# Graph attention on one core: the softmax's second pair of segmented scans replaced by two masked passes with precomputed tables

## The chip, the cores and the metric

The program runs on one core of one Trainium2 chip. The metric is the device time of one execution in microseconds; lower is better. A time given for a version is the median of its runs.

## The reference, cut to what matters

2500 nodes with 512 channels (8 heads of 64), 40000 edges sorted by their destination, two layers of attention over the edges, then a small MLP with layer norms. Everything is float32. The part that the change concerns is the softmax over all edges of one destination:

```python
for l in range(L):
    ...
    a = (q[dst] * k[src]).sum(-1) * scale
    amax = jax.ops.segment_max(a, dst, num_segments=N)
    ...
    e = jnp.exp(a - amax[dst])
    denom = jax.ops.segment_sum(e, dst, num_segments=N)
    alpha = e / (denom[dst] + 1e-16)
    agg = jax.ops.segment_sum(alpha[:, :, None] * v[src], dst, num_segments=N).reshape(N, C)
    x = agg + (x @ Ws[l] + bs[l]) + enc
```

## The kernel before, in words

The edges are cut into 176 steps of 256 edges (two tiles of 128), each step belonging to one block of 128 destination nodes; there are 20 blocks. The program is a sequence of stages with a barrier of all engines behind most of them (`give_back`, L98):

1. `first_keys` (L154) computes the rows k of the first layer, block by block (20 of them): TensorE turns and multiplies, ScalarE takes the high parts, VectorE the low parts (`low_part`, L435) and the results (`take_keys`, L445), and SyncE stores (L260, L263). Between the blocks VectorE builds the tables of steps (`between`, L581): after block 12 it spreads the destination ("key") of every edge, the keys are transposed by TensorE and copied back by ScalarE (L389) as `key_s`, [128 x 2816]. The 128 partitions are 16 chunks of the edge list times 8 heads; the 2816 columns are the edges of a chunk in order. After block 16 `mark_starts` (L556) compares each key with the one ahead of it, after block 17 `scale_starts` (L559) turns the result into 0 or -1e30 (`fresh`), and SyncE stores it to HBM (L271). After the last block `link_chunks` (L561) notes which chunks share a segment with their neighbours. GpSimd has little to do here: one low part (L283), four indirect DMAs and two casts (L292, L293). SyncE ends the stage by waiting for all stores (L272 to L278).
2. `score`, once for each layer, gathers k rows by indirect DMAs from GpSimd's queue (L657) and computes the scores of all edges, `k.edge`.
3. `soften_collect` (L1000), once for each layer, has two parts in one block of engine programs.
   - The softmax (L1293 to L1329): VectorE sorts the scores into chunk order, TensorE transposes them into PSUM (`big`), and VectorE runs two segmented max scans of 2816 columns: `fwd` forward and `bwd` backward, each from PSUM with the flags `fresh` from SBUF (L1303, L1304; all scans have the line of the helper, L1290). The maxima at the chunk ends go through TensorE and two tiny scans over the chunks, and come back as `carry_col`, the value that enters each chunk from either side. Then both long scans are run again, starting from `carry_col` (L1318, L1319), and the maximum of the two is each edge's segment maximum. Six pieces of up to 512 columns follow: maximum (L1325), scores minus maximum (L1329), exponential on ScalarE (L1469), transposition back on TensorE (L1222), copy to `k.edge` on ScalarE (L1475).
   - The collection, 176 steps: GpSimd gathers the v rows of a step by two indirect DMAs of 128 rows of 2 KB each (L657) into a ring of 16 steps. It starts on this at the beginning of the stage, beside the softmax, and waits when all 16 slots are full, until VectorE has used the first. VectorE weighs a step's rows with the exponentials (`weigh`, L1346), makes the one-hot matrices (L1333) and adds the sums to the block (L1360); TensorE multiplies (L1262). In the first layer VectorE also assembles each finished block as the next layer's x (L1382, L1387), and TensorE computes its k rows; SyncE loads what these need.
4. `finish` is the MLP with its norms. There GpSimd also does elementwise work (L1675) beside VectorE's (L1742).

`score` of layer 1 also splits weights on VectorE (L908) beside its gathers. The engines are ordered by semaphores alone; each engine runs its own list of instructions in the order of the code.

## Time and profile before

| what | value |
|---|---|
| runs | 2756.88, 2774.0, 2786.02 us |
| median | 2774.0 us |
| span of the profiled execution | 2242.0 us |
| own time of the profiled execution | not given by the page |
| VectorE (DVE) busy | 2018.6 us, 90% |
| TensorE (PE) busy | 1875.4 us, 84% |
| GpSimd (POOL) busy | 1506.2 us, 67% |
| ScalarE (ACT) busy | 539.5 us, 24% |

The span goes from the first to the last instruction of one profiled execution. The runs are timed from outside and hold what lies around the instructions as well. Times in the rows are in us from the span's start. The two softmax parts lie at 559 to 605 us and 1506 to 1551 us, `first_keys` ends at 98 us.

### The profile page before, as it was taken

Reading aid. Unit: us, or ns where it says so; the run is one execution under the profiler, and the core shown is the slowest. Engines: PE = TensorE matmul, PEld = TensorE weight load, DVE = VectorE, ACT = ScalarE, POOL = GpSimd, SP = SyncE. Lnnn points to the kernel's source line nnn. Section 1 sums busy time; section 2 is a strip of 40 time slices with the busy share of each in tenths; the row PEclk is TensorE's granted clock in tenths of the full one; section 3 lists DMA queues with packets and bytes.
Section 4 is the critical chain, followed back from the end, with each engine's and each line's share of the span. In section 5 each row is a group of like instructions: output and inputs, shape, how many; then the busy total and the mean of one; then the engine's idle time right before and its main releaser. Section 6 shows DMA issues by size and latency. Waiting matters only on the chain. (4 is left out here: it accounts for less than half of the span.)

```text
span 2242.0 us, 30495 instructions
## 1 busy us (share of the span) xinstructions
PE 1875.4 (84%) x7660; PEld 1411.1 (63%) x7661; DVE 2018.6 (90%) x2398; ACT 539.5 (24%) x1070; POOL 1506.2 (67%) x1499
## 2 busy tenths in 40 slices
PE   7699999986489999996999899854998878768997
PEld 6566666663367777774666666633766555557776
DVE  7499999999899999993999999989999888889994
ACT  3133333332311111112333333332111000032222
POOL 1177777775677777774777777757777777657553
PEclk9899999997699999997999999966999999979999
DMA  8688888885778888886888888856777777641111
GB/s 317 241 268 289 291 288 280 287 288 175 223 220 262 264 263 266 263 259 231 248 284 279 291 291 280 286 176 199 211 210 210 210 210 211 186 164 57 57 48 45
DMA packets 201631, 511.52 MB, mean 228 GB/s; under 512 B 37915, under 2 KB 60571, under 8 KB 201190
## 3 DMA queue, kind: packets, MB, share of 16 engines
q0 software_dynamic: 112832, 369.71, 53.7%
q1 hardware_dynamic: 85862, 135.89, 17.6%
q10 hardware_dynamic: 2880, 5.24, 0.7%
q8 instruction: 25, 0.41, 0.1%
q14 instruction: 32, 0.26, 0.0%
HBM read 451.33 MB, written 59.06 MB: 228 GB/s over the span
## 5 line engine op out<-in xcount | busy, mean ns | idle before, releaser
L657 POOL DMA_INDIRECT coll_rows<-v_rows,coll_index x704 | 673.7, 957 | 223.2 <-issue 199.0
L657 POOL DMA_INDIRECT all_work<-k_rows,all_work x704 | 668.7, 950 | 226.8 <-issue 204.1
L1262 PE MATMUL coll_banks<-coll_ev,coll_hot 128*128 128x260 f32 x2816 | 684.8, 390 | 76.1 <-DVE coll_ev L1346 47.9
L1262 PEld LDWEIGHTS coll_banks<-coll_ev,coll_hot 128*128 128x128 f32 x2816 | 517.4, 190 | 222.5 <-DVE coll_ev L1346 99.2
L851 PE MATMUL score_q_ps<-score_q,score_hot 128*128 x1408 | 418.4, 422 | 108.7 <-DVE all_work L879 50.3
L1346 DVE TENSOR_TENSOR coll_ev<-coll_rows,coll_banks 128x1024 f32<-128x1024 f32 x352 | 425.7, 1210 | 38.7 <-DMA coll_rows<-v_rows,coll_index 37.6
L879 DVE TENSOR_TENSOR all_work<-score_q_ps,all_work 128x1024 f32<-128x1024 f32 x352 | 428.8, 1220 | 35.2 <-issue 8.0
L884 DVE TENSOR_REDUCE graph_edge<-all_work 128x1024 f32 (+1 forms) x352 | 421.7, 1208 | 0.0
L851 PEld LDWEIGHTS score_q_ps<-score_q,score_hot 128*128 128x128 f32 x1408 | 268.8, 199 | 214.9 <-issue 164.8
L959 ACT ACTIVATE score_hot<-score_local,all_iota_col 128x512 fp32r<-128x512 uint8 x176 | 127.3, 723 | 613.4 <-DVE all_work L879 581.5
L1360 DVE TENSOR_TENSOR all_work<-all_work,coll_banks 128x520 f32 x352 | 241.7, 687 | 5.5 <-PE coll_banks L1262 5.3
L1513 ACT ACTIVATE coll_ev<-coll_e_now 128x16 f32<-128x16 f32 x352 | 75.2, 215 | 635.9 <-PE coll_banks L1262 635.8
L633 PE MATMUL score_new_q<-graph_wq_hi,score_xt 128*128 128x512 f32 x320 | 109.9, 405 | 29.9 <-DMA score_xt<-x_turned 29.9
L962 ACT ACTIVATE score_hot<-score_hot,all_ones 128x512 fp32r<-128x512 f32 x176 | 127.3, 723 | 5.8
L633 PE MATMUL score_new_skip<-layer_w_skip_hi,score_xt 128*128 128x512 f32 x320 | 121.4, 422 | 1.3 <-DVE score_skip L897 1.3
L1333 DVE TENSOR_TENSOR coll_hot<-coll_banks,coll_local_up 128x512 f32<-128x512 f32 x176 | 119.7, 681 | 0.2
L1663 POOL TENSOR_TENSOR mlp_h_lo<-mlp_h_all,mlp_h_hi 128x512 fp32r<-128x512 f32 x40 | 65.3, 1637 | 72.6 <-ACT mlp_h_hi L1867 68.1
L633 PE MATMUL score_new_v<-layer_w_v_hi,score_xt 128*128 128x512 f32 x320 | 109.4, 403 | 0.0
L633 PEld LDWEIGHTS score_new_q<-graph_wq_hi,score_xt 128*128 128x128 f32 x320 | 62.9, 197 | 45.4 <-DMA score_xt<-x_turned 22.6
L633 PE MATMUL coll_banks<-coll_w_k_hi,coll_xt 128*128 128x512 f32 x160 | 68.4, 470 | 15.7 <-DVE coll_xt L1391 15.7
L633 PEld LDWEIGHTS score_new_skip<-layer_w_skip_hi,score_xt 128*128 128x128 f32 x320 | 63.8, 199 | 24.5 <-issue 9.3
L633 PEld LDWEIGHTS score_new_v<-layer_w_v_hi,score_xt 128*128 128x128 f32 x320 | 60.0, 188 | 20.7 <-issue 9.4
(248 smaller groups left out, 2145.6 us busy)
## 6 DMA issues: line engine op xcount, KB each, us to landing
score_xt<-x_turned SPq DMA_DIRECT2D x42, 512.0 KB, 6.5
all_work<-k_rows,all_work POOLq DMA_INDIRECT x704, 4.9
score_local<-local_dst SPq DMA_DIRECT2D x176, 64.0 KB, 6.3
coll_rows<-v_rows,coll_index POOLq DMA_INDIRECT x704, 3.7
x_turned<-keys_xt SPq DMA_DIRECT2D x20, 512.0 KB, 4.9
score_skip<-in_x SPq DMA_DIRECT2D x40, 256.0 KB, 4.7
v_rows<-score_v_out SPq DMA_DIRECT2D x40, 256.0 KB, 5.1
skip_rows<-score_skip SPq DMA_DIRECT2D x40, 256.0 KB, 4.0
```

The costliest lines, as they stand in the source:

```text
L633: return nc.tensor.matmul(out, xt[:, a, c, :], w[b][:, c, :], start=c == 0 and n == 0, stop=False)
L657: nc.gpsimd.indirect_dma_start(rows[:, slot, t, :], None, table, at).then_inc(arrived[slot], 16)
L851: last = nc.tensor.matmul(q_ps[s % 2][:, t, :], hot[:, s // HOT_STEPS % 2, e:e + P], parts[:, part * C:(part + 1) * C], start=part == 0, s ...
L879: nc.vector.tensor_tensor(prod[:, s % PRODS], q_ps[s % 2][:], rows[:, s % RING], ALU.mult).then_inc(multiplied, 1)
L884: nc.vector.tensor_reduce(k.edge[:, bass.ds(n * TPS, TPS), :], prod[:, s % PRODS].rearrange("p t (h d) -> p t h d", d=D), AX.X, ALU.add).t ...
L959: nc.scalar.activation(hot[:, slot, :], local[:, part, :], ACT.Square, bias=k.iota_col[:, 0:1], scale=-1.0).then_inc(squared, 1)
L962: nc.scalar.activation(hot[:, slot, :], hot[:, slot, :].bitcast(F32), ACT.Relu, bias=k.ones[:, 0:1], scale=-1.0).then_inc(hot_ready, 1)
L1262: last = nc.tensor.matmul(sums[sum_slots[s]][:, part, :], m, ev[:, s % EVS, t, part * AGG // 2:(part + 1) * AGG // 2], start=t == 0, stop= ...
L1333: nc.vector.tensor_tensor(hot[:, slot], iota_ps.unsqueeze(1).to_broadcast([P, n, P]), local_up[:, bass.ds(pair * n, n)].unsqueeze(2).to_br ...
L1346: nc.vector.tensor_tensor(ev[:, s % EVS, :, 0:C].rearrange("p t (h d) -> p t h d", d=D), rows[:, s % V_RING].rearrange("p t (h d) -> p t h ...
L1360: nc.vector.tensor_tensor(at, at, sums[sum_slots[s]], ALU.add).then_inc(added, 1)
L1513: nc.scalar.activation(ev[:, s % EVS, :, C:AGG], e_now[:, h, at * TPS:(at + 1) * TPS, :], ACT.Copy).then_inc(ev_act, 1)
```

## The change

In `first_keys`, GpSimd gets new work once all keys are copied (`keys_copied`): it takes the first and the last key of each chunk (`ends`), and makes two tables of 2816 columns, `of_first` and `of_last`, with 0 where an edge's key is the chunk's first (last) key and -1e30 elsewhere. Each table is two instructions, one compares and scales, one adds -1e30 in place. `of_first` overwrites the buffer `key8_all`, `of_last` overwrites `key_s` and so waits for `mark_starts` and for TensorE's `turn_ends`. SyncE stores both to HBM behind the last block's stores, and waits for them at the end of the stage.

In `soften_collect`, SyncE loads both tables at the start, behind `fresh`. The second of the two remaining long scans, backward, now runs over the result of the first, `fwd` in SBUF, instead of the scores in PSUM, so that `bwd` holds each segment's maximum within its chunk. The second pair of long scans goes. In its place stand two passes for each piece: bwd = max(table + carry, bwd), once with each table and its column of `carry_col`; the subtraction then takes `bwd`. The three are staggered over the pieces.

```diff
+        ends = ph.sb("ends", [P, 2])
+        of_first, of_last = key8_all, key_s
...
@@ first_keys, SyncE: behind the loop over the blocks
+                sp.wait_ge(others_known, 1)
+                sp.dma_start(k.others_d[0], of_first).then_inc(others_out, 16)
+                sp.wait_ge(others_known, 2)
+                sp.dma_start(k.others_d[1], of_last).then_inc(others_out, 16)
...
+                sp.wait_ge(others_out, 32)
@@ first_keys, GpSimd: behind the two casts
+                pool.wait_ge(keys_copied, QUARTS)
+                nc.gpsimd.tensor_copy(ends[:, 0:1], key_s[:, 0:1]).then_inc(ends_taken, 1)
+                nc.gpsimd.tensor_copy(ends[:, 1:2], key_s[:, SLOTS - 1:SLOTS]).then_inc(ends_taken, 1)
+                pool.wait_ge(ends_taken, 2)
+                nc.gpsimd.tensor_scalar(of_first, key_s, ends[:, 0:1], BIG, ALU.is_equal, ALU.mult).then_inc(others_begun, 1)
+                pool.wait_ge(others_begun, 1)
+                nc.gpsimd.tensor_scalar(of_first, of_first, -BIG, None, ALU.add).then_inc(others_known, 1)
+
+                pool.wait_ge(keys_marked, 1)
+                pool.wait_ge(ends_turned, 1)
+                pool.wait_ge(others_known, 1)
+                nc.gpsimd.tensor_scalar(of_last, key_s, ends[:, 1:2], BIG, ALU.is_equal, ALU.mult).then_inc(others_begun, 1)
+                pool.wait_ge(others_begun, 2)
+                nc.gpsimd.tensor_scalar(of_last, of_last, -BIG, None, ALU.add).then_inc(others_known, 1)
@@ first_keys, VectorE: mark_starts
                     link(v.tensor_tensor(fresh[:, 1:SLOTS], key_s[:, 1:SLOTS], key_s[:, 0:SLOTS - 1], ALU.not_equal))
+                    dve.sem_inc(keys_marked, 1)
@@ soften_collect: buffers and SyncE
+        with ExitStack() as early:
+            others = [early.enter_context(nc.sbuf_tensor(f"coll{layer}_others{i}", [P, SLOTS], F32)) for i in range(2)]
...
                 sp.dma_start(fresh[:], k.fresh_d).then_inc(fresh_in, 16)
+                for i in range(2):
+                    sp.dma_start(others[i][:], k.others_d[i]).then_inc(others_in, 16)
@@ soften_collect, VectorE
                 link(scan(fwd[:], before, big[:, 0:SLOTS], -BIG))
-                scan(flip(bwd), flip(after), flip(big[:, 0:SLOTS]), -BIG).then_inc(ends_ready, 1)
+                scan(flip(bwd), flip(after), flip(fwd), -BIG).then_inc(ends_ready, 1)
...
                 link(v.tensor_copy(carry_col[:], cols[:, 0:2]))
-                link(scan(fwd[:], before, big[:, 0:SLOTS], carry_col[:, 0:1]))
-                link(scan(flip(bwd), flip(after), flip(big[:, 0:SLOTS]), carry_col[:, 1:2]))
+                dve.wait_ge(others_in, 32)
...
-                for n in range(QUARTS + 1):
+                for n in range(QUARTS + 2):
                     if n < QUARTS:
                         at = quarters[n]
-                        v.tensor_tensor(fwd[:, at], fwd[:, at], bwd[:, at], ALU.max).then_inc(max_known, 1)
-                    if n > 0:
+                        v.scalar_tensor_tensor(bwd[:, at], others[0][:, at], carry_col[:, 0:1], bwd[:, at], ALU.add, ALU.max
+                                               ).then_inc(first_met, 1)
+                    if 0 < n <= QUARTS:
                         at = quarters[n - 1]
-                        dve.wait_ge(max_known, n)
-                        v.tensor_tensor(fwd[:, at], big[:, at], fwd[:, at], ALU.subtract).then_inc(less_max, 1)
+                        dve.wait_ge(first_met, n)
+                        v.scalar_tensor_tensor(bwd[:, at], others[1][:, at], carry_col[:, 1:2], bwd[:, at], ALU.add, ALU.max
+                                               ).then_inc(max_known, 1)
+                    if n > 1:
+                        at = quarters[n - 2]
+                        dve.wait_ge(max_known, n - 1)
+                        v.tensor_tensor(fwd[:, at], big[:, at], bwd[:, at], ALU.subtract).then_inc(less_max, 1)
```

## Rows read from the trace of the kernel before

**Rows 1.** The page: busy time, share of the span and instructions of each engine

```profile
PE 1875.4 (84%) x7660; PEld 1411.1 (63%) x7661; DVE 2018.6 (90%) x2398; ACT 539.5 (24%) x1070; POOL 1506.2 (67%) x1499
```

**Rows 2.** Windows, layers 0 and 1: us, busy PE, PEld, DVE, ACT, POOL; clock, DMA share

```profile
800.00:900.00 100.00, 96.15 (x431) 78.47 (x430) 98.91 (x139) 15.65 (x58) 75.62 (x81) 1.00 0.84 265
1750.00:1850.00 100.00, 80.25 (x322) 57.49 (x321) 85.82 (x106) 9.56 (x45) 75.63 (x81) 1.00 0.73 210
```

**Rows 3.** VectorE's waits, 605-1016 and 1550-1960 us: total us, times, longest us

```profile
DVE coll_ev L1346 <- DMA coll_rows<-v_rows,coll_index: 1.9, 2, 1.6
...
DVE coll_ev L1346 <- DMA coll_rows<-v_rows,coll_index: 35.7, 70, 0.9
```

**Rows 4.** Timeline (start, us, line, idle before), GpSimd around the first weighing, both layers

```profile
601.78 0.95 POOL L657 DMA_INDIRECT coll_rows<-v_rows,coll_index  x1 [0.30 <-issue]
606.87 0.94 POOL L657 DMA_INDIRECT coll_rows<-v_rows,coll_index  x1 [4.15 <-DVE coll_ev L1346]
...
1553.31 0.94 POOL L657 DMA_INDIRECT coll_rows<-v_rows,coll_index  x1 [3.52 <-DVE coll_ev L1346]
```

**Rows 5.** Timeline, VectorE in the softmax of layer 0

```profile
572.38 6.02 DVE L1290 TENSOR_TENSOR_SCAN coll_bwd<-coll_fresh,coll_banks 128x2816 f32<-128x2816 f32 x1
...
582.73 6.08 DVE L1290 TENSOR_TENSOR_SCAN coll_fwd<-coll_fresh,coll_carry_col,coll_banks 128x2816 f32<-128x2816 f32 x1
...
594.96 1.29 DVE L1325 TENSOR_TENSOR coll_fwd<-coll_fwd,coll_bwd 128x512 f32<-128x512 f32 x2
...
602.03 1.29 DVE L1333 TENSOR_TENSOR coll_hot<-coll_banks,coll_local_up 128x512 f32<-128x512 f32 x2
```

**Rows 6.** The instructions of L1742, 1960 to 2000 us (duration ns min/median/max)

```profile
L1742 DVE SCALAR_TENSOR_TENSOR mlp_y<-mlp_y,mlp_y_scale,mlp_shift x4: 735/741/4993, 1974.3 to 1982.5; 128x512 f32<-128x512 f32 x4
```

**Rows 7.** Timeline, a two-input VectorE instruction and the gather beside it

```profile
1051.35 2.29 DVE L908 TENSOR_TENSOR layer_w_v_lo<-score_w_raw,layer_w_v_hi 128x2048 fp32r<-128x2048 f32 x1 [4.88 <-ACT layer_w_v_hi L967]
...
1051.60 2.86 POOL L657 DMA_INDIRECT all_work<-k_rows,all_work  x1 [0.30 <-issue]
```

**Rows 8.** Timeline, GpSimd's gathers beside the scan and the maximum, layer 0

```profile
572.54 0.95 POOL L657 DMA_INDIRECT coll_rows<-v_rows,coll_index  x1 [0.30 <-issue]
...
595.07 1.40 POOL L657 DMA_INDIRECT coll_rows<-v_rows,coll_index  x1 [0.30 <-issue]
```

**Rows 9.** Timeline, the backward scan and the gathers beside it, layer 1

```profile
1518.84 6.02 DVE L1290 TENSOR_TENSOR_SCAN coll_bwd<-coll_fresh,coll_banks 128x2816 f32<-128x2816 f32 x1
...
1518.40 0.95 POOL L657 DMA_INDIRECT coll_rows<-v_rows,coll_index  x1 [0.30 <-issue]
1519.65 0.95 POOL L657 DMA_INDIRECT coll_rows<-v_rows,coll_index  x1 [0.30 <-issue]
```

**Rows 10.** Timeline, the end of the first stage: ScalarE, VectorE, SyncE

```profile
77.05 0.86 ACT L389 COPY all_work<-keys_big 128x512 f32<-128x512 f32 x2 [2.49 <-PE keys_big L329]
...
81.16 3.08 DVE L556 TENSOR_TENSOR all_work<-all_work 128x2815 f32<-128x2815 f32 x1
...
85.49 1.62 DVE L559 TENSOR_SCALAR all_work<-all_work 128x2815 f32<-128x2815 f32 x1
...
91.63 0.33 SPq L263 DMA_DIRECT2D k_rows<-keys_k_out  x1
```

**Rows 11.** SyncE's wait at the end of the first stage, and the transfers there (windows)

```profile
SPq L275 <- DMA k_rows<-keys_k_out: 5.2, 1, 5.2
...
90.00:92.00 2.00, 0.80 (x4) 0.34 (x2) 1.09 (x4) 0.00 (x0) 0.00 (x0) 1.00 1.08 437
92.00:94.00 2.00, 0.00 (x0) 0.00 (x0) 1.90 (x12) 0.00 (x0) 0.00 (x0) 1.00 0.95 395
```

**Rows 12.** Groups of instructions on GpSimd: one input, and two inputs

```profile
L292 POOL CAST keys_sdst_f<-keys_sdst_i 128x512 f32<-128x512 int32 x1 | 0.6, 611 | 5.5 <-DMA keys_sdst_i<-in_dst,keys_row_i 5.5
L283 POOL TENSOR_TENSOR graph_wq_lo<-keys_raw,graph_wq_hi 128x2048 fp32r<-128x2048 f32 x1 | 4.6, 4618 | 14.9 <-ACT graph_wq_hi L384 14.9
```

**Rows 13.** Issues of the flags' load: count, size, median us from issue to landing

```profile
coll_fresh<-segment_starts SPq DMA_DIRECT2D x2, 1408.5 KB, 6.2
```

More of the change, by code:

```diff
@@ L221, in first_keys @@
         ends_turned, fresh_known, fresh_out = ph.sem("ends_turned"), ph.sem("fresh_known"), ph.sem("fresh_out")
+        keys_marked, ends_taken, others_begun, others_known, others_out = (
+            ph.sem(n) for n in ("keys_marked", "ends_taken", "others_begun", "others_known", "others_out"))
         TABLES_AT, KEYS_AT, ENDS_AT = 11, 13, 16
@@ L1014, in soften_collect @@
         e_now = ph.sb("e_now", [P, 2, HALF * TPS, HEADS])
+        assert HOTS * HOT_STEPS * TPS * P + EVS * TPS * AGG + 2 * HALF * TPS * HEADS >= 2 * SLOTS
         src_up = ph.sb("src_up", [P, TILES], I32)
@@ L1059, in soften_collect @@
         carry_ready, carry_turned = ph.sem("carry_ready"), ph.sem("carry_turned")
-        max_known = ph.sem("max_known")
+        first_met, max_known, others_in = ph.sem("first_met"), ph.sem("max_known"), ph.sem("others_in")
         less_max, raised, back, steps = ph.sem("less_max"), ph.sem("raised"), ph.sem("back"), ph.sem("steps")
@@ L1977, in graph_attention @@
     k.skip_d = [nc.dram_tensor(f"skip_rows{layer}", [ROWS, C], F32).ap() for layer in range(LAYERS)]
+    k.others_d = [nc.dram_tensor(f"other_segments{i}", [P, SLOTS], F32).ap() for i in range(2)]
     k.fresh_d = nc.dram_tensor("segment_starts", [P, SLOTS + 1], F32).ap()
```

## The prediction

> **What bounds the kernel now.** I read the page's busy times first, then windows of the collections, then the waits, and only then the softmax itself. The page makes VectorE look like the bound: 90% busy against 67% for GpSimd [rows 1]. But the issuing of an indirect DMA counts as 0.95 us with 0.30 us of uncounted gap behind it, one every 1.25 us [rows 4, 8, 9]. So GpSimd with 75.6 us busy in 100 and 81 records is saturated: 80 gathers x 1.25 us = 100 us [rows 2]. In layer 1 VectorE is busy only 85.8 us in 100 there and waits 70 times for gathered rows; in layer 0, at 98.9 us in 100, it is behind at first and waits for rows only in the last steps, just catching up at the end [rows 2, 3]. Both collections thus end when the last of 352 gathers has come, and the stage lasts as long as the chain of gathers: 352 x 1.25 = 440 us plus whatever holds GpSimd up.
>
> What has the softmax to do with this? Gathers run beside it until the ring's 16 slots are full, 32 gathers x 1.25 us = 40 us. Then GpSimd waits for VectorE's first weighing: an idle time of 4.15 us in layer 0 and of 3.52 us in layer 1, less the usual gap of 0.30, so 3.85 and 3.22 us [rows 4]. This is all that a shorter softmax can give back, however much VectorE is relieved.
>
> **The change part by part.**
>
> Second pair of scans, on VectorE. The first starts at 582.73 and the maxima behind the pair at 594.96: 12.2 us go in each layer [rows 5]. The six maxima and six subtractions lasted from 594.96 to 602.03, 7.1 us, or 0.61 us for each full piece. Six more instructions, five of 512 and one of 256 columns, add 5 x 0.61 + 0.35 = 3.4 us. A scalar_tensor_tensor of this shape takes 0.735 us undisturbed [rows 6] against the 0.68 us recorded for the others, so 18 of them may cost 0.5 us more. VectorE is relieved of about 8.5 us a layer, 17 us in both. Of this 3.85 + 3.22 = 7.1 us reach the chain of gathers.
>
> The backward scan reading SBUF. Its length should stay 6.0 us. What changes is its second input: flags and data now both lie in SBUF. The trace shows what such an instruction does to gathers [rows 7]: VectorE's subtraction of two SBUF tensors ends at 1051.35 + 2.29 = 1053.64; the gather begun at 1051.60 takes 2.86 us instead of 0.95 and ends at 1054.46, 0.82 us after it. Beside a scan with one input in PSUM the gather of 572.54 takes its plain 0.95 us [rows 8]. The short case agrees: the gather of 595.07 begins 0.11 us into the first of two maxima over SBUF tensors and takes 1.40 us [rows 8]. So a gather seems to need something early, about 0.95 - 0.82 = 0.13 us after its start, which VectorE holds for the whole instruction. Applied to the new scan: in layer 0 it runs from 572.38 to 578.40; the gather of 572.54 would end at 579.22 instead of 573.49, a loss of 5.7 us. In layer 1 the gather of 1518.40 gets through before the scan starts at 1518.84, and that of 1519.65 would end at 1524.86 + 0.82 = 1525.68, a loss of 5.1 us [rows 9]. If scans hold nothing, the loss is 0; it cannot exceed the scan's 6.0 us. I take 5.7 and 5.1, since the mechanism is shown at 2.3 us and at 0.68 us with the same instructions on GpSimd.
>
> The new passes over SBUF. Twelve instead of six instructions a layer with two SBUF inputs, now in the pattern pass, pass, subtraction (the last reads PSUM). Stepping a gather every 1.25 us through this pattern of 0.61 us pieces with the rule above loses 2.1 to 3.0 us a layer, depending on where the first falls; I take 2.5. The six maxima of before cost 1.40 - 0.95 = 0.45 us in layer 0 [rows 8], and I let layer 1 have as much. Net +2.1 a layer; bounds -0.5 and +3.
>
> Sum for the collections: layer 0: -3.85 + 5.7 + 2.1 = +4.0 us, less 0.5 us since VectorE then ends right behind the gathers and not 0.5 us later: +3.5. Layer 1: -3.2 + 5.1 + 2.1 = +4.0. Together +7.5 us.
>
> The Trainium skill, page "SBUF — State Buffer", section "Who interferes with whom", says two things: a VectorE instruction with two SBUF inputs contends with a GpSimd instruction that reads SBUF, and a tensor_tensor did not stall DMAs issued there, because writing descriptors needs the other, write, interface. By its second sentence the gathers go on and the sum has no 5.7, 5.1 and 2.1; the stalled gather of [rows 7] speaks for the first sentence.
>
> Loading the two tables. SyncE issues them right behind `fresh`, 1408 KB each like that, which lands 6.2 us after its issue [rows 13]; they must be there at 582.7, 23 us after. Their bytes compete with the gathers, so they may be some us late. VectorE has room: it would reach the first weighing near 596, while the ring, with a chain 8 us slower, is full only near 609. Up to 12 us of lateness cost nothing; if the tables took longer, each us beyond would count. I take 0.
>
> The tables in `first_keys`. The keys are copied at 77.9 [rows 10]. One-input work on GpSimd took 0.61 us for 512 columns, about 1.0 ns a column behind a start of 0.1 us; two-input work 2.26 ns a column [rows 12]. For 2816 columns this gives 2.9 us or 6.4 us for each of the four instructions; I take 3.5, near the first, as they have one tensor input but two operations and a pointer. They meet VectorE's L556 (two SBUF inputs) and L559 [rows 10], and I let each wait for the other in turn: GpSimd 78.3 to 81.9, L556 until 84.9, GpSimd until 88.5, L559 (85.5 before) until 90.1, GpSimd until 97.2. L559 ends 3.0 us later than before, and so does the low part queued behind it on VectorE, which TensorE needs for the last block's product. Then the stores: SyncE ended its wait 5.2 us behind the issue at 91.96, at 97.2 [rows 10, 11], with the engines moving 437 and 395 GB/s on the way. Two tables of 1.44 MB at 420 GB/s, about their mean, are 6.9 us more. `fresh` is stored 2 to 3 us later, so the transfers start later too, and the end comes at about 105: +8 us. Nothing hides this: the barrier stands behind it and `score` begins after it. Bounds: +6.3 (transfer alone at 460 GB/s) and +17 (6.4 us an instruction: tables ready at 108.8, landed 5.4 us later).
>
> The Trainium skill, "GPSIMD Engine Reference", section 3.1, measured 769 ns for 512 elements in a tight loop; by it (estimate) an instruction takes 4.2 us and the stage 2 to 3 us more than I take. No row here shows such a tensor_scalar on GpSimd.
>
> Whole sum: +8 + 7.5 = +15.5 us. The page gives only a span, 2242.0, with 532 us between it and the median; I take that part as unchanged. 2242 becomes 2257.5, and 2774 becomes 2789.
>
> **The rivals.**
>
> A, VectorE is the bound: its full 17 us come off, and the tables hide behind other work: 2757. For it: 98.9 us busy in 100 in layer 0. Against: 70 waits for rows in layer 1 and the saturated chain of gathers.
>
> B, neither scan nor passes hold the gathers: the collections give back 7.1 + 0.5 us, the first stage costs 8: 2774. Against it stands the stalled gather [rows 7]; for it, that no row shows a scan with two full SBUF inputs. The Trainium skill's sentence on tensor_tensor, page "SBUF — State Buffer", quoted above, would make this come true.
>
> C, GpSimd builds the tables at the two-input rate: first stage +17, collections +7.5: 2798. It decides from about 3.8 us an instruction on, where the last table is ready later than the stores of the first are through.
>
> D, the tables do not shorten VectorE's part at all, because they land after 595: then GpSimd's idle time stays as well, 7.1 us, and the time is 2796. Against: a load of this size lands 6.2 us after its issue [rows 13], beside gathers that leave a quarter of the engines' share free in layer 1 (0.73) [rows 2].
>
> **How the numbers follow.** Forecast 0.52, C 0.18, B 0.18, A 0.06, D 0.06. All lie within 1% (27.7 us, about what a measurement of this kernel can tell from no change) of 2774. The runs of before scatter over 29 us though, so C with a measurement some us high would pass the upper bound, and A with one some us low the lower. The range goes from 2764 (B with 10 us of the runs' scatter; A stays out) to 2808 (C with 10 us of scatter). Faster by over 1%: 0.04; within 1%: 0.83; slower by over 1%: 0.13.
>
> **What would show it.** In the profile of after: one gather of about 6.7 us in layer 0 and one of 6.0 us in layer 1, each ending 0.8 us behind the backward scan, and several of 1.2 to 1.5 us beside the passes; no idle time of GpSimd at the first weighing; VectorE's first weighing near 596 but the last gather of layer 0 some 4 us later, measured from the stage's start. VectorE would show more waits for gathered rows than 2 in layer 0. The first stage would end near 105, with four GpSimd instructions of 3 to 4 us. It is wrong if the long gathers are missing (B), or if the stages shrink by 8 us each (A).

## The result, and the profile after

The changed kernel took 2804.7 us (median of 4 runs, 2798.0 to 2816.2), the kernel before 2776.2 us beside it (2756.9 to 2786.0): ratio 1.0102, 95% interval 1.0065 to 1.0140, so 28 us slower (18 to 39).

Before anything else the two profiles have to be made comparable. Here are the span and the clock from the view of the cores, first of the profile shown of before:

```profile
core 0: 2242.0 us, clock 0.942
```

of the same kernel profiled again (e1 below):

```profile
core 0: 2760.8 us, clock 0.852
```

and of after:

```profile
core 0: 2796.2 us, clock 0.848
```

The same program has two spans 519 us apart. The run that belongs to the second took 2762.6 us, 1.8 us more than its span, and that of after 2798.0 us, again 1.8 more. So the 532 us between the span of the first profile and the median do not lie around the instructions. The runs of the experiments came from three chips, and the kernel before took 2752 us on one, 2782 us on another and 2243 us on the third: by its span the first profile shows a chip of the third kind (this is inferred, as that profile has no time of its own), the times of before and after come from the other kind. I call them the slow and the fast chips. VectorE's, ScalarE's and GpSimd's instructions are as long on either (VectorE is busy for 2018.6 us in the first profile and 2016.5 us in before again). TensorE's are not: its busy time is 1875.4 and 2062.3 us, the mean of its collection's matmul (L1262) 390 and 429 ns, at a lower granted clock. That is at most 187 of the 519 us; the rest is idle time. The 519 us lie in the stages that gather:

```
us                     before, shown   before again   after
first_keys ends             98.7           97.4       120.0
score, layer 0             460.8          577.4       582.4
softmax, layer 0            45.4           50.8        38.0
collection, layer 0        412.0          553.0       571.6
score, layer 1             471.5          577.4       584.9
softmax, layer 1            44.5           50.7        40.1
collection, layer 1        404.5          550.3       557.6
mlp                        286.1          282.8       282.3
```

(Softmax: from VectorE's sorting of the scores to the first weighing; collection: from there to the last; the mlp from there to the end; the short pieces between collection and score are left out.) After against before again: the first stage lost 22.6 us, the softmax gained 12.8 and 10.6, and the collections lost 18.6 and 7.3. The sum is 25 us, beside 35 between these two spans, most of the rest being in the scores; single runs of one kernel on one chip scatter by 30, and the two profiles need not be of the same chip.

The first stage, timeline of after:

```profile
77.52 9.77 POOL L307 TENSOR_SCALAR all_work<-all_work,keys_ends 128x2816 f32<-128x2816 f32 x1
80.30 7.99 DVE L579 TENSOR_TENSOR all_work<-all_work 128x2815 f32<-128x2815 f32 x1
...
87.38 8.10 POOL L309 TENSOR_SCALAR all_work<-all_work 128x2816 f32<-128x2816 f32 x1
...
89.64 7.32 DVE L583 TENSOR_SCALAR all_work<-all_work 128x2815 f32<-128x2815 f32 x1
...
95.67 10.90 POOL L314 TENSOR_SCALAR all_work<-all_work,keys_ends 128x2816 f32<-128x2816 f32 x1 [0.19 <-POOL all_work L309]
...
104.29 0.43 SPq L277 DMA_DIRECT2D other_segments<-all_work  x1
...
106.66 7.32 POOL L316 TENSOR_SCALAR all_work<-all_work 128x2816 f32<-128x2816 f32 x1
106.74 7.30 DVE L599 TENSOR_SCALAR graph_link_f<-graph_link_f 1x128 f32<-1x128 f32 x1
...
114.00 0.33 SPq L279 DMA_DIRECT2D other_segments<-all_work  x1
...
120.02 0.20 POOL L668 COPY all_work<-graph_src_t 128x16 int32<-128x16 int32 x1 [6.04 <-POOLq L98]
```

GpSimd needs 7.3 to 10.9 us for each table instruction, where I took 3.5. VectorE's comparison, 3.08 us in [rows 10], takes 7.99, its scaling 7.32 instead of 1.62, and an instruction on 128 elements of one partition 7.30 instead of 0.21, ending with GpSimd's. Other instructions of VectorE beside the tables keep their length: those with an operand in PSUM take 0.67 to 0.69 us there as elsewhere. The last table is ready at 113.98, and its store sets the end of the stage.

The softmax of layer 0, the backward scan and the gathers beside it (VectorE, then GpSimd), and the same gather in layer 1:

```profile
714.76 6.02 DVE L1319 TENSOR_TENSOR_SCAN coll_bwd<-coll_fresh,coll_fwd 128x2816 f32<-128x2816 f32 x1
...
725.12 1.42 DVE L1353 SCALAR_TENSOR_TENSOR coll_bwd<-coll_others,coll_carry_col,coll_bwd 128x512 f32<-128x512 f32 x2
...
736.06 1.29 DVE L1367 TENSOR_TENSOR coll_hot<-coll_banks,coll_local_up 128x512 f32<-128x512 f32 x2
740.04 0.29 DVE L1373 COPY coll_banks<-graph_edge 128x128 f32<-128x128 f32 x1 [2.69 <-ACT graph_edge L1509]
```
```profile
714.20 0.95 POOL L681 DMA_INDIRECT coll_rows<-v_rows,coll_index  x1 [0.30 <-issue]
715.45 6.09 POOL L681 DMA_INDIRECT coll_rows<-v_rows,coll_index  x1 [0.30 <-issue]
721.85 0.94 POOL L681 DMA_INDIRECT coll_rows<-v_rows,coll_index  x1 [0.30 <-issue]
723.09 1.03 POOL L681 DMA_INDIRECT coll_rows<-v_rows,coll_index  x1 [0.30 <-issue]
...
1929.24 6.73 POOL L681 DMA_INDIRECT coll_rows<-v_rows,coll_index  x1 [0.30 <-issue]
```

One gather in each layer is held until 0.76 us behind the scan (715.45 + 6.09 = 721.54 against 714.76 + 6.02 = 720.78), where [rows 7] gave 0.82 (in layer 1 the scan runs from 1929.19 to 1935.21, the gather until 1935.97). Beside the passes nearly all gathers take 0.95 to 1.04 us, and one in each layer 1.35. The passes, from 725.12 to the subtraction's end at 735.96, are 10.8 us. No wait for the tables shows.

### The profile page after: what moved, and what is told of

Read it like the earlier page. It is cut to its first block and busy times, and to the rows that moved or that the text cites. A ratio compares the mean times of both kernels' runs of the same rounds, so it can differ in the third digit from the quotient of the medians.

```text
span 2796.2 us, 30521 instructions
## 1 busy us (share of the span) xinstructions
PE 2085.3 (75%) x7660; PEld 1560.4 (56%) x7661; DVE 2020.9 (72%) x2406; ACT 535.0 (19%) x1070; POOL 1559.5 (56%) x1505
## 5 line engine op out<-in xcount | busy, mean ns | idle before, releaser
L1291 PE MATMUL coll_banks<-coll_ev,coll_hot 128*128 128x260 f32 x2816 | 768.7, 431 | 262.7 <-DVE all_work L1394 99.2
L681 POOL DMA_INDIRECT coll_rows<-v_rows,coll_index x704 | 688.4, 978 | 452.2 <-issue 231.4
L1291 PEld LDWEIGHTS coll_banks<-coll_ev,coll_hot 128*128 128x128 f32 x2816 | 595.2, 216 | 417.5 <-issue 159.8
L875 PE MATMUL score_q_ps<-score_q,score_hot 128*128 x1408 | 478.4, 470 | 228.3 <-DVE all_work L903 140.4
L875 PEld LDWEIGHTS score_q_ps<-score_q,score_hot 128*128 128x128 f32 x1408 | 299.9, 224 | 366.8 <-issue 311.1
L1394 DVE TENSOR_TENSOR all_work<-all_work,coll_banks 128x520 f32 x352 | 243.6, 692 | 359.1 <-DMA k_rows<-keys_k_out 247.8
L657 PE MATMUL score_new_q<-graph_wq_hi,score_xt 128*128 128x512 f32 x320 | 123.8, 451 | 39.8 <-DMA score_xt<-x_turned 39.8
L657 PE MATMUL score_new_skip<-layer_w_skip_hi,score_xt 128*128 128x512 f32 x320 | 133.2, 460 | 1.8 <-issue 1.7
L657 PE MATMUL coll_banks<-coll_w_k_hi,coll_xt 128*128 128x512 f32 x160 | 76.3, 521 | 54.8 <-DVE coll_xt L1425 52.0
L657 PEld LDWEIGHTS score_new_q<-graph_wq_hi,score_xt 128*128 128x128 f32 x320 | 72.0, 225 | 59.5 <-DMA score_xt<-x_turned 31.7
L657 PEld LDWEIGHTS score_new_skip<-layer_w_skip_hi,score_xt 128*128 128x128 f32 x320 | 70.9, 222 | 28.0 <-issue 11.7
L657 PEld LDWEIGHTS score_new_v<-layer_w_v_hi,score_xt 128*128 128x128 f32 x320 | 64.4, 201 | 22.6 <-issue 9.6
```

The costliest lines, as they stand in the source:

```text
L657: return nc.tensor.matmul(out, xt[:, a, c, :], w[b][:, c, :], start=c == 0 and n == 0, stop=False)
L681: nc.gpsimd.indirect_dma_start(rows[:, slot, t, :], None, table, at).then_inc(arrived[slot], 16)
L875: last = nc.tensor.matmul(q_ps[s % 2][:, t, :], hot[:, s // HOT_STEPS % 2, e:e + P], parts[:, part * C:(part + 1) * C], start=part == 0, s ...
L1291: last = nc.tensor.matmul(sums[sum_slots[s]][:, part, :], m, ev[:, s % EVS, t, part * AGG // 2:(part + 1) * AGG // 2], start=t == 0, stop= ...
L1394: nc.vector.tensor_tensor(at, at, sums[sum_slots[s]], ALU.add).then_inc(added, 1)
```

## The experiments

Each was timed in 5 rounds, 4 to 12 runs of it. Differences in us are the ratio's, with its 95% interval, on the median of before on that chip: 2752 us for the first four, 2782 us for the next four (both slow chips), 2243 us for the last four (the fast chip).

**e1, the kernel before again.** No edit.

> The kernel before, unchanged, measured against itself, and a second profile of it. Ratio 1.000 within 0.3%. Its first profile had a span of 2242 us while the runs take 2776, and the kernel after has a span of 2796 us at a run of 2798. Theory 1 (the first profile of before was of an unusually undisturbed execution): the new span is 2765 to 2785 us, and engines stand idle for some hundred us more than in the first profile, mostly in the steps of score and collection. Theory 2 (the change itself made the 554 us of idle time in the profile): the span is 2242 again. The first stage should end at 98 to 99 us as before (GpSimd's copy of L644 starts it).

Measured: 1.0015 (0.9982 to 1.0048), span 2760.8 us. Theory 1 holds as to the span; that the first profile came from another kind of chip, and not from a rare execution, is what the later comparisons add: all 11 runs of before on the fast chip took 2234 to 2247 us.

**e2, the tables without the new softmax.**

```diff
-                for i in range(2):
-                    sp.dma_start(others[i][:], k.others_d[i]).then_inc(others_in, 16)
...
+                link(scan(fwd[:], before, big[:, 0:SLOTS], carry_col[:, 0:1]))
+                link(scan(flip(bwd), flip(after), flip(big[:, 0:SLOTS]), carry_col[:, 1:2]))
```

> Tables built and stored in the first stage as in the change, but never loaded; the softmax is that of before. The first profile of after shows the first stage ending 21 us later (120.0 instead of 98.7 us), with four GpSimd instructions of 7.3 to 10.9 us. Theory (the first stage is the larger part of the loss): 21 us over before, ratio 1.0077. Rival (the loss lies in the collections, the first stage's end is made up for later): under 7 us, ratio below 1.0025.

Measured: +19.8 us (12.1 to 27.2); the first stage ends at 120.7. The theory holds: the tables alone carry most of the loss.

**e3, the backward scan from PSUM in the changed kernel.** The two directions are not joined within a chunk.

```diff
-                scan(flip(bwd), flip(after), flip(fwd), -BIG).then_inc(ends_ready, 1)
+                scan(flip(bwd), flip(after), flip(big[:, 0:SLOTS]), -BIG).then_inc(ends_ready, 1)
```

> The change with one edit: the remaining backward scan reads the scores from PSUM as in the kernel before, so VectorE's 6 us instruction has one input in SBUF. It leaves out the joining of the two scans within a chunk, so that the maxima are partial ones. Theory (a scan with both inputs in SBUF holds up the gathers): no gather of 5 to 7 us beside the scan, and up to 5.7 + 5.1 = 10.8 us less than after where GpSimd's chain of gathers is the bound, ratio about 1.006 to 1.008; with much idle time elsewhere in the stage, less. Rival (gathers are not the bound in an ordinary execution): the long gathers go but the time stays that of after, 1.010.

Measured: +20.9 us (13.8 to 28.1), where the changed kernel itself is at 28 and, in e5, at 20. The gathers beside the scan are back at 0.95 us, so the hold-up is that of the second SBUF input. The number is the theory's against the first and the rival's against the second: the price can't be told from this run.

**e4, the tables on VectorE.** One instruction for each table, no work for GpSimd.

```diff
+                    v.tensor_scalar(of_first, key_s, ends[:, 0:1], -BIG, ALU.not_equal, ALU.mult).then_inc(others_known, 1)
...
+                    v.tensor_scalar(of_last, key_s, ends[:, 1:2], -BIG, ALU.not_equal, ALU.mult).then_inc(others_known, 1)
```

> The change with the tables made on VectorE, one instruction each (not equal, times -1e30) instead of four on GpSimd. By the row of L559 (1.62 us for 2815 columns) the two cost 3.2 us of VectorE, undisturbed by GpSimd. Theory (GpSimd's slow table instructions are the loss of the first stage, and not the stores): the first stage ends 7 to 9 us later than before (106 to 108 us), and the time is 12 to 14 us below after, ratio 1.005 to 1.006. Rival (the two stores of 1.44 MB are the loss): the stage ends at 115 us or later.

Measured: +11.3 us (3.9 to 19.0); the stage ends at 107.6, 10.2 us later than in e1. In the timeline of e4 the same comparison that GpSimd does in 9.77 us is:

```profile
83.53 1.69 DVE L567 TENSOR_SCALAR all_work<-all_work,keys_ends 128x2816 f32<-128x2816 f32 x1
```

The rival is refuted. A little over half of the first stage's loss, 12 of 23 us, was thus GpSimd's. And 11.3 less 10.2 leaves 1 us (with the interval's 7 us on either side) for everything in the softmax and the collections, though the first weighing comes 11 us sooner there in each layer.

**e5, the changed kernel again.** No edit, second chip.

> The changed kernel, nothing altered, to stand beside the others of this batch. Both theories: 26 to 30 us over the kernel before, ratio near 1.010 (the earlier comparison gave 1.0102).

Measured: +20.3 us (13.4 to 27.3), less than expected; the stage ends at 120.4 us. The loss is thus known as 28 us (18 to 39) and as 20 us (13 to 27) from two comparisons.

**e6, the new softmax without the tables' making.**

```diff
-                    sp.dma_start(others[i][:], k.others_d[i]).then_inc(others_in, 16)
+                    sp.dma_start(others[i][:], k.fresh_d[:, 0:SLOTS]).then_inc(others_in, 16)
```

and the first stage of before.

> First stage as before (no tables built or stored), softmax as after; both masked passes read the flags of the segment starts in the tables' place, with loads of the same size, so the joining of segments across chunks is left out in substance and kept in time. The first stage must end near 97 us again. Theory S (my prediction's account of the collections): 7.5 us slower than the kernel before, ratio 1.003. Theory V (VectorE is the bound in an ordinary execution, nothing holds the gathers): 17 us faster, ratio 0.994. Theory N (the collections give the 11 us of a layer's softmax back elsewhere, as the profiles of after and of the variant with tables from VectorE suggest): within 4 us of the kernel before.

Measured: +7.0 us (-0.3 to +13.9), the stage's end back at 98.6. Theory V is refuted. S (7.5 us) fits best, but the interval holds part of N's 4 us too.

**e7, e6 with the backward scan from PSUM** (the edit of e3).

> As softmax only, and the backward scan reads the scores in PSUM instead of the forward scan's result in SBUF, which leaves the joining of the two directions out. No gather is held up beside that scan (0.95 us each instead of one of 6.1 and one of 6.7 us). Theory S (the chain of gathers is the bound, also in an ordinary execution): 10.8 us faster than softmax only, ratio 0.996 against it. Rival (VectorE, with its own delays, is the bound by then, and the ring makes the loss up before its end): within 3 us of softmax only.

Measured: -5.0 us (-12.5 to +2.8), so 12 us under e6, with some 10 us of uncertainty. VectorE's scan and GpSimd's gathers in e7, in their timelines:

```profile
696.17 6.02 DVE L1295 TENSOR_TENSOR_SCAN coll_bwd<-coll_fresh,coll_banks 128x2816 f32<-128x2816 f32 x1
```
```profile
696.42 0.95 POOL L657 DMA_INDIRECT coll_rows<-v_rows,coll_index  x1 [0.30 <-issue]
697.67 0.95 POOL L657 DMA_INDIRECT coll_rows<-v_rows,coll_index  x1 [0.30 <-issue]
```

and in e6, where the scan ends at 694.03:

```profile
688.06 6.72 POOL L657 DMA_INDIRECT coll_rows<-v_rows,coll_index  x1 [0.30 <-issue]
695.08 0.94 POOL L657 DMA_INDIRECT coll_rows<-v_rows,coll_index  x1 [0.30 <-issue]
```

The mechanism is shown: the second SBUF input holds the gather. Its price of 10.8 us fits this pair; e3 against e5 and the first comparison of after gives between 0 and 7. I take it as likely, with the size open.

**e8, no second pair at all.** The chunks are not joined.

```diff
-                link(scan(fwd[:], before, big[:, 0:SLOTS], carry_col[:, 0:1]))
-                link(scan(flip(bwd), flip(after), flip(big[:, 0:SLOTS]), carry_col[:, 1:2]))
```

> The kernel before without its second pair of long scans and with nothing in their place: the maxima and all that follows run on the first pair's results, so the joining across chunks is left out. VectorE has 12.2 us less in each layer, and nothing is added anywhere. Theory S (chain of gathers bound): only GpSimd's idle time at the first weighing and 0.5 us come back, 7.6 us in all, ratio 0.9972. Theory V (VectorE bound): 24.4 us, ratio 0.991. Theory N (something else fixes the length of the collections): within 3 us of before.

Measured: +3.3 us (-3.1 to +10.0). VectorE has 24.4 us less to do, and nothing comes back: theory S (7.6 us faster) and theory V (24.4 us faster) lie outside the interval, and N's "within 3 us" fits. The timeline of ScalarE in the softmax of layer 0 shows why, beside TensorE's, VectorE's and GpSimd's:

```profile
715.48 0.63 ACT L1467 ACTIVATE coll_bwd<-coll_fwd 128x512 f32<-128x512 f32 x1
724.76 0.60 ACT L1473 ACTIVATE graph_edge<-coll_banks 128x512 f32<-128x512 f32 x1 [8.65 <-DMA keys_bias_k<-in_bk]
725.26 0.62 ACT L1467 ACTIVATE coll_bwd<-coll_fwd 128x512 f32<-128x512 f32 x1
735.28 0.60 ACT L1473 ACTIVATE graph_edge<-coll_banks 128x512 f32<-128x512 f32 x1 [9.40 <-DMA keys_bias_k<-in_bk]
```
```profile
713.67 3.60 PE L1222 MATMUL coll_banks<-all_ident,coll_bwd 128*128 128x128 f32 x12 [2.84 <-issue]
725.93 1.12 PE L1222 MATMUL coll_banks<-all_ident,coll_bwd 128*128 128x128 f32 x4 [8.65 <-ACT coll_bwd L1467]
```
```profile
738.89 0.29 DVE L1337 COPY coll_banks<-graph_edge 128x128 f32<-128x128 f32 x1 [19.49 <-ACT graph_edge L1473]
```
```profile
730.38 0.95 POOL L657 DMA_INDIRECT coll_rows<-v_rows,coll_index  x1 [0.30 <-issue]
741.25 0.94 POOL L657 DMA_INDIRECT coll_rows<-v_rows,coll_index  x1 [9.93 <-DVE coll_ev L1344]
```

L1473 waits for one thing, TensorE's transpositions (the releaser that the row names is from the first stage and can't be it). Twelve of them, three pieces, run from 713.67 and have ended by 717.27, the second piece by about 716.1. ScalarE starts on the second piece at 724.76 and on the third at 735.28, after idle times of 8.65 and 9.40 us. GpSimd issues its gathers every 1.25 us until 731.33. The trace's records of that semaphore itself have the second and third signal at 724.74 and 735.26 us. So TensorE's signals come that late, and VectorE stands idle for 19.49 us. A low clock alone does not do it: in this softmax the granted clock is 0.53 in before again and 0.55 in the first profile, which has no late signal.

**e9, the second pair twice.**

```diff
+                link(scan(fwd[:], before, big[:, 0:SLOTS], carry_col[:, 0:1]))
+                link(scan(flip(bwd), flip(after), flip(big[:, 0:SLOTS]), carry_col[:, 1:2]))
```

> The kernel before with its second pair of long scans done twice over: 12.2 us more on VectorE in each layer, 24.4 in all, and nothing else. The counterpart to the run without the pair. Theory L (the length of the softmax on VectorE counts in one direction only: in ordinary executions the first weighing comes near 50 us after the stage's start, because TensorE's semaphores for the transpositions back come late, and VectorE stands idle 7 to 8 us ahead of it): the first 7 us a layer vanish in that idle time, the rest counts, about 9 to 12 us slower, ratio 1.004. Rival V (each us on VectorE counts): 24.4 us slower, ratio 1.009. Rival N (not even lengthening counts): within 3 us.

Measured, on the fast chip: +24.0 us (20.6 to 27.6). There rival V's number holds, but that number is also what the chain of gathers gives for a softmax that gets longer: GpSimd waits all of it. Its idle time is 16.57 - 0.31 = 16.3 us, 12.4 us more than the 3.85 us of [rows 4]:

```profile
601.24 0.94 POOL L657 DMA_INDIRECT coll_rows<-v_rows,coll_index  x1 [0.31 <-issue]
618.75 0.94 POOL L657 DMA_INDIRECT coll_rows<-v_rows,coll_index  x1 [16.57 <-DVE coll_ev L1348]
```

Theory L was made for a slow chip, where this wasn't run: open.

**e10, no second pair, and the gathers only behind the softmax.** As e8, and:

```diff
+                pool.wait_ge(e_known, QUARTS)
                 gather_rows(nc, k, pool, k.v_d, rows, src_up[:], index, TURNS - 1, first_index,
```

> The kernel before without the second pair, and GpSimd starts the gathers of the v rows only when ScalarE has put the last piece of the exponentials back, so that none runs beside the softmax. Theory G (TensorE's late semaphores come with the gathers): the idle time of 19 us on VectorE ahead of the first weighing goes, the last exponentials are back about 35 us after the stage's start instead of 50, and the first weighing waits for its own gather, about 40 us after the start; the whole is longer, since 32 gathers no longer run beside the softmax. Rival T (the delays come by the clock of the machine, whatever GpSimd does): the last exponentials are still back only near 50 us after the start.

Measured, on the fast chip: +55.4 us. The last exponentials are back 32.5 us after the stage's start, the 44.9 of before less 12.2 and little more. But there is no late signal on this chip with gathers either, so the run can't tell theory G from T. It shows that on the fast chip gathers cost the softmax nothing, and that running them beside it is worth about 28 us a layer (55.4 / 2), or more if leaving out the pair gave something back.

**e11, only the two stores.**

```diff
+                sp.wait_ge(keys_copied, QUARTS)
+                sp.dma_start(k.others_d[0], key_s).then_inc(others_out, 16)
+                sp.dma_start(k.others_d[1], key_s).then_inc(others_out, 16)
```

> The kernel before, and SyncE stores two tables of 1.44 MB from SBUF at the end of the first stage, where the changed kernel stores its own; no table is computed, none is loaded. My term for the transfers: the first stage ends 6 to 7 us later, at 103.5 to 104.5 instead of 97.4, and the whole is 6 to 7 us slower, ratio 1.0025. Rival (the stores run beside the stage's last waits and cost nothing): within 2 us.

Measured, on the fast chip: +7.0 us (4.3 to 9.6), the stage ends at 106.5 beside 98.7 in the first profile. SyncE's waits in e11, with total, times and longest in us:

```profile
SPq L280 <- DMA other_segments<-all_work: 6.6, 1, 6.6
```

My 6.9 us for the transfers are right.

**e12, the tables alone and late.** Computed as in the changed kernel, not stored, with one more wait on GpSimd:

```diff
                 pool.wait_ge(keys_copied, QUARTS)
+                pool.wait_ge(fresh_known, 1)
```

> The tables alone: GpSimd computes them as in the changed kernel, but begins only when VectorE has finished scaling the flags; they are neither stored nor loaded, and the softmax is that of before; the first stage waits for the last table. Theory O (7.3 us is GpSimd's own time for such an instruction on 2816 columns; only the excess over it, 9.8 and 10.9 us, came from VectorE's work beside it): four instructions of 7.3 to 8 us, and VectorE's comparison and scaling are back at 3.1 and 1.6 us. Rival P (the time is long because VectorE and GpSimd hold each other up): four instructions near 3.5 us each. By theory O the stage ends near 118 us, and the whole is some 20 us slower.

Measured, on the fast chip: +25.8 us (22.2 to 29.2), the stage ends at 123.3. Its timeline, GpSimd and VectorE:

```profile
80.68 3.08 DVE L576 TENSOR_TENSOR all_work<-all_work 128x2815 f32<-128x2815 f32 x1
...
85.12 1.62 DVE L580 TENSOR_SCALAR all_work<-all_work 128x2815 f32<-128x2815 f32 x1
...
87.29 9.77 POOL L304 TENSOR_SCALAR all_work<-all_work,keys_ends 128x2816 f32<-128x2816 f32 x1
...
97.15 7.33 POOL L306 TENSOR_SCALAR all_work<-all_work 128x2816 f32<-128x2816 f32 x1
...
97.23 7.32 DVE L596 TENSOR_SCALAR graph_link_f<-graph_link_f 1x128 f32<-1x128 f32 x1
...
104.67 9.80 POOL L311 TENSOR_SCALAR all_work<-all_work,keys_ends 128x2816 f32<-128x2816 f32 x1 [0.19 <-POOL all_work L306]
...
114.55 7.32 POOL L313 TENSOR_SCALAR all_work<-all_work 128x2816 f32<-128x2816 f32 x1
```

Rival P is refuted. Theory O holds in that the time is GpSimd's own, and fails in calling the excess over 7.3 us VectorE's: 9.8 us is GpSimd's own time for the instruction with a pointer and two operations, 7.3 us for the in-place addition, with nothing large of VectorE's beside them. What VectorE added in the changed kernel is 0.8 us (8.10 us) and 1.1 us (10.90 us). And the tiny L596 (97.23 + 7.32 = 104.55) ends only when GpSimd's instruction beside it does (97.15 + 7.33 = 104.48).

**Where the softmax's 11 us go.** From the starts of the weighings in each profile, in us after the start of the stage, layer 0:

```
weighing number        1    3    5    9   21   41   81  176
before, fast chip     45   48   53   64   92  137  231  457
e9, fast chip         57   60   67   77  105  150  244  469
before again (e1)     51   54   59   76  110  181  309  604
after                 38   41   65   75  118  180  310  610
e4                    40   42   65   75  115  177  303  595
e6                    40   43   63   74  118  180  313  610
e7                    50   53   60   74  110  173  305  611
e8                    51   54   59   74  108  171  304  602
```

On the fast chip the 12 us of e9 stay in every column. On the slow ones the first weighing comes at 38 to 51, and the ninth at 74 to 76 in every kernel of the table. In after it is VectorE's wait right behind the third (timelines of VectorE and TensorE):

```profile
743.24 1.21 DVE L1380 TENSOR_TENSOR coll_ev<-coll_rows,coll_banks 128x1024 f32<-128x1024 f32 x1
757.98 0.70 DVE L1394 TENSOR_TENSOR all_work<-all_work,coll_banks 128x520 f32 x1 [13.53 <-DMA k_rows<-keys_k_out]
```
```profile
741.69 5.55 PE L1291 MATMUL coll_banks<-coll_ev,coll_hot 128*128 128x260 f32 x16 [3.55 <-issue]
758.82 1.64 PE L1291 MATMUL coll_banks<-coll_ev,coll_hot 128*128 128x260 f32 x3 [11.58 <-issue]
```

L1394 takes a sum that TensorE had finished by 747.24, and starts at 757.98 (the row's releaser, a store, is none that it waits for). What e8 loses ahead of the first weighing, after loses a step or two behind it.

## Why the prediction was right or wrong

The time, 2804.7, lies within the range of 2764 to 2808, near its upper end; the loss of 28.5 us is a hair over the 27.7 that I drew as the line of 1%, to which I gave a chance of 0.13. The forecast of 2789 was 16 us short, that of the difference, +15.5, some 13 us by the first comparison and 5 by e5, whose interval holds it. By its own steps:

- **The tables in `first_keys`: +8, measured +21 to +23.** This is the step that failed, and it is the whole miss: the term "I take 3.5, near the first" for GpSimd's instruction. I had GpSimd at work from 78.3 to 97.2 us; it worked from 77.5 to 114.0, and its four instructions sum to 36.1 us instead of 14. The rows of one-input work that I scaled from were a plain cast; with a scalar operand and two operations 2816 columns cost 9.8 us and the in-place addition 7.3. Rival C had the kind (it decides from 3.8 us on) and the lower part of the size: 6.4 us, +17. The estimate by the Trainium skill, "GPSIMD Engine Reference", section 3.1, of 4.2 us was too short as well; the trace decides. My picture of the turns that VectorE and GpSimd take was also too mild: I gave VectorE's last part 3 us of delay; it lost 4.9 and 5.7 us on two instructions and 7.1 on one of 128 elements. The last block's store, which waits for VectorE, is issued at 103.92 instead of 91.63 us. The transfers' 6.9 us were right (e11: 7.0). Of the result's 28 us, e2 gives this stage 20, and e6 the rest 7.
- **The softmax and collections: +7.5, measured +7.0 in e6.** The sum is right, but by parts of which two were off (below): what was to come back, 7.1 us, did not, and the passes held the gathers by less. They were off in opposite ways, and the account is of a chip on which gathers are the bound, so that the sum fits is in part luck.
- **The backward scan holds a gather: right.** Gathers of 6.09 and 6.73 us, where I had 6.7 and 6.0 (which layer gets the longer one depends on where the scan falls between two gathers); 0.76 us behind the scan instead of 0.82; gone with PSUM as the input (e3, e7). Rival B is refuted as to the scan. The Trainium skill, page "SBUF — State Buffer", section "Who interferes with whom", has it that a tensor_tensor did not stall DMAs issued from GpSimd; [rows 7] shows one with two SBUF operands that did (2.86 us instead of 0.95), and the rows of e6 and e7 show the same of a scan.
- **The passes hold gathers by 2.5 us a layer: too much.** The recorded gathers sum to about 0.8 us a layer; on VectorE the passes took 10.8 us where 7.1 + 3.9 = 11.0 were predicted (my 18 slower instructions are 12: two for each of six pieces).
- **The tables are there in time: right.** D is refuted.
- **"Both collections end when the last of 352 gathers has come": right on the fast chip, wrong on the chips that gave the times.** From 800 to 900 us of before again the windows show GpSimd at 60.08 us and 61 records instead of the 75.6 and 81 of [rows 2]:

```profile
800.00:900.00 100.00, 75.97 (x291) 59.70 (x290) 71.28 (x99) 9.76 (x40) 60.08 (x61) 0.88 0.62 187
```

  and its waits (total, times, longest) hold a line of 234.6 us for VectorE's weighing; the first profile has no such line among its three longest:

```profile
POOL coll_rows L657 <- DVE coll_ev L1346: 234.6, 82, 10.2
```

- **What a shorter softmax gives back: 7.1 us, measured nothing (e8: +3.3, -3.1 to +10.0).** I had this at GpSimd's idle time at the first weighing. The interval excludes 7.1 us. On a slow chip that idle time is larger, and still nothing comes back, since the delays of TensorE's signals move in behind it.
- **A, the full 17 us: refuted** by e6 and e8.
- **"532 us between it and the median, taken as unchanged": wrong as a description.** It did little harm, as the largest terms are lengths of VectorE's and GpSimd's instructions, the same on either chip; but the account of the collections was drawn from a chip on which the runs were not made.

No variant beats the kernel before. The best of the new softmax, e7, is level with it, and it makes no tables and does not join the scan directions; e8 leaves little to look for, since even leaving out the whole second pair gains nothing on these chips. What the changed kernel would take on the fast chip was not measured.

## What to carry to other kernels

Price an elementwise instruction on GpSimd from a row of the same form (scalar operand, number of operations), and allow for some of VectorE's SBUF-only instructions beside it lasting as long as GpSimd's; the four table instructions here cost twice what the stage's whole new traffic did. A second SBUF operand on a long VectorE instruction holds the gather that GpSimd is issuing until it ends. And compare the profile's span with the runs before reading a bound from it: where they differ by more than a few us, the profile shows another situation than the times.

## What the runs showed of the hardware that I had not expected

- GpSimd's tensor_scalar on 2816 f32 columns: 9.77 to 9.80 us with a per-partition operand and two operations (3.5 ns a column), 7.32 us for one operation in place with an immediate (2.6 ns a column), against 1.69 us for the first on VectorE.
- A VectorE instruction of 128 elements on one partition took 7.3 us instead of 0.21 beside such a GpSimd instruction. It is not the size of VectorE's work that decides: in after, VectorE's instructions with an operand in PSUM kept 0.69 us there, and two comparisons of 128 elements in SBUF 0.27 and 0.28 us, though one of these took 3.10 us in e12. What does decide was not tried.
- The same program takes 2243 us on one chip and 2752 and 2782 us on two others, with equally long instructions but TensorE's, at a granted clock of 0.94 and 0.85. On the two, in the stages that gather, TensorE's signals come some us late, in the collections about every 20 to 28 us (in before again TensorE, VectorE and ScalarE stand idle together from 760.9, 786.9, 812.0 and 838.5 us on, for 3 to 7 us each); the first stage and the mlp show none of it. The cause is open: the lower clock goes along with it, and which of the two comes first is not shown; that gathers bring it about was to be tried by e10, and wasn't, as that run fell on the chip that doesn't have it.
